# Stacks of a block-sparse cross-attention rebuilt through DRAM, with a reordered projection and the second normalization on GpSimd

## What is computed

```python
# cut to what matters; S = 512, 4 blocks of 128 per sequence, 16 heads of 16
x = _layernorm(x + causal_attention(x, Wq, Wk, Wv, Wo))             # "x1" below
Q, K, V = x @ Wq.T + bq, ctx @ Wk.T + bk, ctx @ Wv.T + bv           # per head: 512 x 16
loc_p   = softmax(Qb @ Kb.T / 4)                # a block of queries on its own block of keys
cross_p = softmax(Qb @ K[i-1, i, i+1].T / 4)    # and on the window of up to three blocks
out = loc_p @ Vb + cross_p @ V[i-1, i, i+1]
x = _layernorm(x + out @ Wo.T + bo)                                 # "x2" below
top2 gates = softmax(top_k(x @ gate_w + gate_b, 2))
x = _layernorm(x + sum_e gate_e * ffn_e(x) + ffn_shared(x))
```

## Time and profile before

| | us |
|---|---|
| median of 3 runs | 947.11 |
| lowest, highest | 946.44, 954.42 |
| the profiled execution | 951.36 |
| its span | 949.6 |

### The profile page before, as it was taken

One profiled execution on the slowest core, in us unless ns is written; L12 is line 12 of the kernel. 1 busy time (PEld: TensorE's weight loads), 2 busy tenths in 40 slices (PEclk: granted clock), 3 DMA queues, 4 the chain that ended last, 5 costly groups with the idle time before them and its releaser, 6 DMA issues. The chain is left out here.

```text
span 949.6 us, 15805 instructions
## 1 busy us (share of the span) xinstructions
PE 823.4 (87%) x5054; PEld 627.7 (66%) x5055; DVE 416.6 (44%) x766; ACT 344.3 (36%) x894; POOL 226.7 (24%) x250
## 2 busy tenths in 40 slices
PE   6584999789998789898949999899999999999940
PEld 5463867585768566765749999577777777777630
DVE  5735475657465846462457553222222222222216
ACT  2120363334352445155155431233333333333313
POOL 5902030204020210000023775411111111111116
PEclk9885999797898999899979999999999999999975
DMA  9911202130122132110073112551011111111025
GB/s 308 148 44 48 65 27 56 50 79 1 29 63 51 40 108 51 45 26 4 1 297 132 56 56 58 200 189 53 30 33 33 33 33 33 33 33 33 22 94 189
DMA packets 59127, 68.47 MB, mean 72 GB/s; under 512 B 18288, under 2 KB 43760, under 8 KB 58960
## 3 DMA queue, kind: packets, MB, share of 16 engines
q1 hardware_dynamic: 55680, 58.61, 21.7%
q0 software_dynamic: 3408, 9.34, 2.7%
HBM read 38.23 MB, written 16.59 MB: 58 GB/s over the span
## 5 line engine op out<-in xcount | busy, mean ns | idle before, releaser
L1567 PE MATMUL ps<-we,hT 128*128 x624 | 142.8, 382 | 2.5 <-ACT hT L722 2.5
L1567 PEld LDWEIGHTS ps<-we,hT 128*128 128x128 f32 x624 | 119.7, 192 | 35.5 <-issue 20.9
L1547 PE MATMUL ps<-we,xT 128*128 x312 | 140.6, 593 | 1.9 <-issue 1.9
L928 DVE TENSOR_REDUCE mx<-ps 128x4 f32<-128x512 f32 (+1 forms) x128 | 102.5, 822 | 62.5 <-PE ps L1381 61.4
L1127 DVE COPY hp<-ps 128x512 f32<-128x512 f32 x78 | 50.3, 686 | 158.4 <-PE ps L1547 158.4
L722 ACT ACTIVATE hT<-ps,b1T 128x128 f32<-128x128 f32 x312 | 84.9, 383 | 35.2 <-PE ps L1558 35.2
L1547 PEld LDWEIGHTS ps<-we,xT 128*128 128x128 f32 x312 | 56.2, 190 | 58.1 <-issue 58.1
L1381 PE MATMUL ps<-k_stack,q_stack 96*128 96x256 f32 (+1 forms) x256 | 74.2, 378 | 16.7 <-DVE mx L928 7.4
L621 ACT ACTIVATE pT<-ps 128x256 f32<-128x256 f32 x128 | 49.3, 385 | 104.4 <-PE ps L1396 96.9
L546 ACT ACTIVATE xT<-ps 128x256 f32<-128x256 f32 x39 | 14.9, 385 | 180.9 <-PE ps L1530 180.9
L1381 PEld LDWEIGHTS ps<-k_stack,q_stack 96*128 96x128 f32 x256 | 42.2, 206 | 46.2 <-issue 22.3
(11 more groups left out here) (212 smaller groups left out, 1265.5 us busy)
## 6 DMA issues: line engine op xcount, KB each, us to landing
we<-in_w SPq DMA_DIRECT2D x16, 1024.0 KB
k_stack<-k_s SPq DMA_DIRECT2D x96, 64.0 KB, 2.0
q_stack<-q_s SPq DMA_DIRECT2D x192, 32.0 KB, 2.0
slot_rows<-attn SPq DMA_DIRECT2D x1, 4992.0 KB, 25.7
xs<-slot_rows SPq DMA_DIRECT2D x39, 128.0 KB, 2.1
yl<-pair_out SPq DMA_DIRECT2D x4, 1024.0 KB, 8.9
x_raw<-in_xT SPq DMA_DIRECT2D x4, 512.0 KB, 4.0
X<-in_x SPq DMA_DIRECT2D x4, 512.0 KB, 7.1
```

Of the source, the lines that this page charges most:

```text
L928: nc.vector.tensor_reduce(mx[:, n, 2 * p:2 * p + 2, r0:r0 + nb], ps[:, 2 * (u % 2):2 * (u % 2) + 2, 0:nb * P].rearrange("p h (b k) -> p h ...
L1547: m = nc.tensor.matmul(ps[:, 2 + c, :], xT[:, q, k, :], w[:, bass.ds(e, 1), k * HID + c * 512:k * HID + (c + 1) * 512].rearrange("p o n -> ...
L1567: m = nc.tensor.matmul(ps[:, 6, 0:D], hT[:, c, :], w[:, bass.ds(e, 1), KD * HID + c * D:KD * HID + (c + 1) * D].rearrange("p o n -> p (o n)"),
```

## The change

Six things change together.

1. SP writes the high and low part of the keys and queries of a half to DRAM (`k_rows`, `q_rows`: two DMAs of 512 KB, `rows_away`) and reads the stacks back from there: 3 DMAs of 256 KB for keys, and 12 of 64 KB for queries, in two groups of two pairs. Unit 0 waits for the keys and the first six, unit 8 for the other six. The block-1 rows are written right behind the stacks of the first half.
2. `project2`: x2 is transposed late, after the third projection, and its logits come after the fourth; `turn_out` comes before the values; the 24 matmuls at its end become 10, except in the prologue.
3. DVE's statistics and its normalization of x1 are laid out row by row over the units of the second half (`norms`).
4. x2 is normalized on POOL: a subtraction, a product and the copy, each over 128 x 1024 (`norm_x2`), after the context's split.
5. Five such matmuls stand before the second half's wait for the residual sums (`WARM_G`).
6. In batch 3 the transposes of the output come ahead of x2's, and five more matmuls stand before its gates.

The core of the diff:

```diff
 WARM = 24
 WARM_B = 16
+WARM_Q = 10
+WARM_G = 5
 WARM_E = 20
 ROW = D + 2
 PARTS = ((0, 0), (0, 1), (1, 0))
 PAIRS = HALF // 2
-PAIR_DMAS = 3 + 2 * 3
+STACK_DMAS = 3 + 2 * 3
+LATE_DMAS = 2 * 3
...
-            def stack(h):
-
-                for g in range(PAIRS):
-                    for sec, part in enumerate((0, 1, 0)):
-                        sp.dma_start(k_stack[32 * sec:32 * sec + 32, h * PAIRS + g, :].bitcast(F),
-                                     k_s[32 * g:32 * g + 32, h, part, :].bitcast(F)).then_inc(stacked[g], 16)
-                    for head in (2 * g, 2 * g + 1):
+            def rows_away(b, h):
+
+                sp.wait_ge(s["qk2_lo"], 4 * b + 2 * h + 1)
+                sp.dma_start(k_rows[h].rearrange("l p t -> p l t"), k_s[:, h, :, :].bitcast(F)).then_inc(k_away[h], 16)
+                sp.wait_ge(s["qk2_lo"], 4 * b + 2 * h + 2)
+                sp.dma_start(q_rows[h].rearrange("l p t -> p l t"), q_s[:, h, :, :].bitcast(F)).then_inc(q_away[h], 16)
+
+            def stack(b, h):
+
+                sp.wait_ge(k_away[h], 16 * b + 16)
+                for sec, part in enumerate((0, 1, 0)):
+                    sp.dma_start(k_stack[32 * sec:32 * sec + 32, h * PAIRS:(h + 1) * PAIRS, :].bitcast(F),
+                                 k_rows[h, part].rearrange("(g p) t -> p g t", g=PAIRS)).then_inc(stacked[h], 16)
+                sp.wait_ge(q_away[h], 16 * b + 16)
+                for part_done, g0 in ((stacked, 0), (stacked_late, PAIRS // 2)):
+                    for par in range(2):
                         for sec, part in enumerate((0, 0, 1)):
-                            r = 32 * sec + 16 * (head % 2)
-                            sp.dma_start(q_stack[r:r + 16, h * HALF + head, :].bitcast(F),
-                                         q_s[16 * head:16 * head + 16, h, part, :].bitcast(F)).then_inc(stacked[g], 16)
+                            r = 32 * sec + 16 * par
+                            at = h * HALF + 2 * g0 + par
+                            sp.dma_start(q_stack[r:r + 16, at:at + HALF // 2 - 1:2, :].bitcast(F),
+                                         q_rows[h, part].rearrange("(g a p) t -> a p g t", g=PAIRS, a=2)
+                                         [par][:, g0:g0 + PAIRS // 2, :]).then_inc(part_done[h], 16)
...
-                sp.wait_ge(s["qk2_lo"], 4 * b + 2)
+                if not first:
+                    sp.wait_ge(stacked[1], 16 * STACK_DMAS * b)
+                rows_away(b, 0)
                 if first:
                     sp.wait_ge(s["masks"], 1)
                 else:
                     sp.wait_ge(s["b_ps"], 2 * UNITS * (2 * b - 1))
-                stack(0)
+                stack(b, 0)
+                rows_away(b, 1)
...
+                stack(b, 1)
...
-            def keep(b, c, bias):
-
-                pool.wait_ge(s["ln_out"], c + 1)
-                Xb = X[:, bass.ts(b, NT), :]
-                if bias:
-                    nc.gpsimd.tensor_tensor(Xb, res[:, 0, :, :], brow[:, 2:3, :].broadcast_to([P, NT, D]), ALU.add)\
-                        .then_inc(s["x_kept"], 1)
-                else:
-                    nc.gpsimd.tensor_copy(Xb, res[:, 1, :, :]).then_inc(s["x_kept"], 1)
+            def keep_x1(b):
+
+                pool.wait_ge(s["x1_out"], b + 1)
+                nc.gpsimd.tensor_tensor(X[:, bass.ts(b, NT), :], res[:, 0, :, :],
+                                        brow[:, 2:3, :].broadcast_to([P, NT, D]), ALU.add).then_inc(s["x_kept"], 1)
+
+            def norm_x2(g, c):
+
+                pool.wait_ge(s["ln_pow"], c + 1)
+                rows = res[:, 1, :, :]
+                nc.gpsimd.tensor_tensor(rows, rows, mv[:, :, 0:1].broadcast_to([P, NT, D]), ALU.subtract)\
+                    .then_inc(s["x2_sub"], 1)
+                pool.wait_ge(s["x2_sub"], g + 1)
+                nc.gpsimd.tensor_tensor(rows, rows, rstd[:, :].unsqueeze(2).broadcast_to([P, NT, D]), ALU.mult)\
+                    .then_inc(s["x2_out"], 1)
+                pool.wait_ge(s["x2_out"], g + 1)
+                nc.gpsimd.tensor_copy(X[:, bass.ts(g, NT), :], res[:, 1, :, :]).then_inc(s["x_kept"], 1)
...
+                if not last:
+                    norm_pow(1 if first else 2 * b)
+                    keep_x1(b + 1)
+
+                    split(c_s, c_raw, (("w1_ps", 2 * b + 4), ("c_raw_in", 16 * b + 32)), "ctx_hi", "ctx_lo", b + 1)
                 if not first:
-                    norm_pow(2 * b)
-                    keep(b - 1, 2 * b, False)
-                if not last:
-                    norm_pow(2 * b + 1)
-                    keep(b + 1, 2 * b + 1, True)
-
-                    split(c_s, c_raw, (("w1_ps", 2 * b + 4), ("c_raw_in", 16 * b + 32)), "ctx_hi", "ctx_lo", b + 1)
+                    c = 2 * b if last else 2 * b + 1
+                    norm_pow(c)
+                    norm_x2(b - 1, c)
...
-                    if j == 0 and g is not None:
-                        gate_rows(g, 0)
                     if j == 1:
                         act.wait_ge(s["ctx_lo"], b + 1)
                         for i in range(2):
                             act.wait_ge(s["v2_ps"], 2 * b + i + 1)
                             copy(v_wait[:, 2 * i:2 * i + 2, :], ps[:, 4 + i, :].rearrange("p (n d) -> p n d", n=2), "v2_out")
...
+                    if j == 2 and g is not None:
+                        gate_rows(g, 4)
...
+            def norms(u, c1, c2, done):
+
+                if u == 0:
+                    dve.wait_ge(s["ln_res"], done)
+                stats1, var1, rows1 = ((0, 1, 2, 3), 4, (6, 7, 8, 10)) if c1 is not None else ((), None, ())
+                stats2, var2 = (((5, 11, 12, 13), 14) if c1 is not None else ((0, 1, 2, 3), 4)) if c2 is not None else ((), None)
+                if u in stats1:
+                    norm_stat(stats1.index(u), 0, c1 if u == stats1[-1] else None)
+                if u in stats2:
+                    norm_stat(stats2.index(u), 1, c2 if u == stats2[-1] else None)
+                if u == var1:
+                    norm_var(c1)
+                if u == var2:
+                    norm_var(c2)
+                if u in rows1:
+                    norm_x1(rows1.index(u), c1)
...
-                    if j == 0 and g is not None:
-                        gate_logits(g, 3)
                     if j == 1 and c is not None:
                         if g is None:
                             dve.wait_ge(s["pad_out"], 32)
-                        else:
-                            gates(g, 3)
                         combine(c, 0)
+                if g is not None:
+                    gate_logits(g, 7)
+                    gates(g, 7)
...
-                half(2 * b + 1, 2 * b, 1, (() if first else ((2 * b, 1),)) + (() if last else ((2 * b + 1, 0),)))
+                glue_and_attention1(None if first else b - 1, None if last else b + 1, 1 if first else 2 * b)
+                half(2 * b + 1, 2 * b, 1, (1, None, 2) if first else (None, 2 * b, 2 * b + 1) if last
+                     else (2 * b, 2 * b + 1, 2 * b + 2))
...
-                if n is not None:
-                    pe.wait_ge(s["ln_res"], cn + 1)
-                elif cg is not None:
-                    pe.wait_ge(s["ln_res"], cg + 1)
+                if g is not None and n is not None:
+                    keep_clock(WARM_G)
+                pe.wait_ge(s["ln_res"], done)
...
-                pe.wait_ge(s["ln_out"], cn + 1)
+                pe.wait_ge(s["x1_out"], b + 1)
                 turn(4, rows_of_res(0), "x1_ps")
-                if g is not None:
-                    turn(0, rows_of_res(1), "g_ps")
                 for j, blk in enumerate((0, 0, 1, 1)):
                     if j == 0:
                         pe.wait_ge(s["ctx_lo"], b + 1)
@@ -1325,21 +1372,25 @@
                         m = mm3(pe, ps[:, 7 - j % 2, :], lambda l: w[:, 1 - j % 2, l, k, blk * P:(blk + 1) * P],
                                 lambda l: src[:, l, k, :], k == 0, k == KD - 1)
                     m.then_inc(s["qk2_ps"], 1)
-                    if j == 0 and g is not None:
-                        gate_logits(g, 3)
                     if j == 1:
-                        rows_of(4, c_s, w, 2, "v2_ps")
-                        if g is not None:
-                            gates(g, 3)
-                            pe.wait_ge(s["lgT_out"], g + 1)
                         if c is not None:
                             pe.wait_ge(s["augT_out"], c + 2)
                             turn_out(c)
-                pe.wait_ge(s["v2_out"], 2 * b + 2)
-                keep_clock(WARM)
+                        rows_of(4, c_s, w, 2, "v2_ps")
+                    if j == 2:
+                        pe.wait_ge(s["v2_out"], 2 * b + 2)
+                        if g is not None:
+                            pe.wait_ge(s["x2_out"], g + 1)
+                            turn(4, rows_of_res(1), "g_ps")
+                if g is not None:
+                    pe.wait_ge(s["qk2_lo"], 4 * b + 3)
```

(22 more changed lines are left out.)

109 lines of the change are left out of this document (56 added, 53 removed).

## The result

The changed kernel took 963.2 us (median; 961.9 to 964.4), the kernel before 948.2 beside it: a ratio of 1.0146, 95% interval 1.0096 to 1.0197. The change makes the kernel slower by about 1%; 937 was forecast. Medians and ranges here are of all executions, but a ratio counts only those within 1.5% of the kernel's fastest, which leaves out one of four of e3 and of e10, one of ten of f2 and four of ten of f4 (the profiled one among them), each 5 to 13 us above its kernel's median. The profiled execution took 962.15 us, its span is 960.4, its mean granted clock 0.897 (0.929 before).

The account below looks back on a forecast made before the run. PE, busy 87% of the span, was taken to set the time in most stages. The terms summed to -14.8 from the profiled 951.4 us: 936.6, say 937, with a range of 924 to 952.

Parts of the forecast that it names:

- Batch 0's half: First half of batch 0: no more waits for pairs, shorter aug rows, 15.4 us instead of 24.8; taken as -9.0.
- its own marks: Signs for batch 0 in the changed profile: unit 0 at 65 to 66 us, aug transposes near 81.
- Projection of batch 1: Ahead of batch 1's first half: fourteen matmuls fewer, but stacks ready only at 9.0 us; -2.0, the wait uncovered.
- First halves of batches 1, 2, 3: POOL's split of x moves ahead of the end, so all three take 22.2 us; -1.7.
- the round trip is late and the half starts cold: Rival: stacks via DRAM come at 15 us instead of 9, halves start at lower clock; 965 us, chance 0.08.
- Projections of batches 2, 3: From aug transposes to unit 0: shorter waits and fewer warm matmuls, -4.0 and -4.5, 1 added for ws; together -7.5.
- Second halves: POOL's x2 operations hold DVE's aug steps, transposes at 27.2 us: batch 1 -1.9, batch 2 +4.3; batches 0, 3 together -0.4.
- End of attention: After the last half nothing covers x2's normalization on POOL, and everything of the experts waits: +3.4.
- Glue: Stretch between the two halves of a batch, four times: forecast difference 0.

Follow-up runs that it names:

- e3: The kernel before with the stacks through DRAM alone, 24 warm matmuls kept: 942.3 us, ratio 0.9865.
- e10: The changed kernel with x2 normalized on DVE, the ws loads behind batch 3's stacks, and 10 warm matmuls: median 925.8 us, ratio 0.9732.
- f2: The changed kernel with x2's normalization on DVE alone, 10 warm matmuls and early ws loads kept: 942.9 us, ratio 0.9923.
- f4: The changed kernel with 14 warm matmuls for 10, nothing else: 949.1 us, ratio 0.9945.
- e7: The kernel before with stacks through DRAM and the two ws loads issued behind batch 3's stacks: 938.8 us, ratio 0.9855.
- f3: The changed kernel with only the ws loads moved behind batch 3's stacks: 940.4 us, ratio 0.992.
- e6: The changed kernel with 24 warm matmuls and x2 normalized on DVE, its copy staying on POOL: 939.1 us, ratio 0.9868.
- e1: The changed kernel with 24 warm matmuls again instead of 10 ahead of the first halves of batches 1 to 3: 950.0 us, ratio 1.0013.

## Why the prediction failed, step by step

**Batch 0's half** (-9.0): right, -9.3, with its own marks: unit 0 at 65.6, transposes at 81.1.

**Projection of batch 1** (-2.0): the wait was forecast as 1.3 us and was 1.5; the group came 9.6 us after SP issued the store instead of 9.0: the store was as taken, the last landing 2.5 us later, the six issues 1.5 shorter. The size was right. What it led to was not.

**First halves of batches 1, 2, 3** (-1.7, all at 22.2): this is the step that failed, by 28 us. The working counted the wait as its own length and said that it "is covered by nothing". A wait of 0.8 to 5.5 us cost its length and 9.3 more, because the half behind it ran at 1.2 GHz to its end: 31.5 us for 22.2. Part of the 9.3 comes back in the glue that follows. After h2 and h4 it took 27.6 to 28.0 us behind five of seven cold halves, 29.6 and 29.8 behind the other two, and 28.9 to 30.3 behind a warm one; after h6 20.6 to 21.0 behind a cold and 22.2 to 23.4 behind a warm one. I had the case among the rivals, "the round trip is late and the half starts cold", but asked for an idle time of 5 us, and gave it 3 us a half. Its first half, the late round trip, happened only in batch 3. The second half needs no late round trip. The sign was in the rows: the earlier trace rows showed a half at 0.53, and the earlier trace rows that it took 29.1 for 22.9. The trace has waits of 1.25, 0.70 and 1.43 us in it, and the clock fell 0.9 us behind the last. I read it as one execution's accident that the change would remove. Accident it was in part, since batch 2's half has the same three waits and stayed warm; but every such wait runs that risk, and the change put one in front of three halves.

**Projections of batches 2, 3** (-7.5): -2.5. The terms as listed take 4.5 off each, which gives 17.9 for batch 2 and not the 18.4 that was written. Batch 2 took 19.0. Batch 3 took 23.7, because the store behind 2 MB of loads landed after 8.4 us; 1 us was allowed for it. e7 and f3 show it: with the loads behind the stacks the wait is gone.

**Second halves** (-1.9, +4.3): -3.3 and +2.9, right in kind. Both took 25.8 us for the 27.2 taken, mainly since POOL's subtraction and product take 1.90 us, and not the 2.37 of a sum of the same size. One aug step was caught by each, as the working had it, and the low clock of h3 did not come back. e6 prices the lock by taking POOL's operations away: 3.3 us a half. The Trainium skill, "SBUF — State Buffer", section "SBUF: two separate sides", has the rule that the prediction used: the engine that comes second to the shared port pair waits for the whole operation of the first. DVE's rows of 2.06, 1.88 and 1.85 us, each with its POOL row, agree.

**End of attention** (+3.4): +4.0; 3.2 of it goes when x2 is back on DVE (e6). PE waits 2.5 us for POOL there, and part of the rest is clock: x2's transposes and logits behind the wait take 1.62 and 1.04 us, for 1.06 and 0.62 before.

**Glue** (0): -6.3, not foreseen, 3.2 and 2.7 of it behind the cold h2 and h6: the mean clock there is 1.00, where it was 0.87 and 0.86 before. Behind the cold h4 it is 0.90 for 0.91, and the glue 0.2 longer. Where it comes, it is the other side of the same cost.

Without the cold halves the sum would have held roughly: +10.8 less 28.3 for the halves, and 3 to 5 back for the glue (an estimate from the two ranges above), is -14.5 to -12.5 against -14.8. That is partly luck: the projections of batches 2 and 3 were 5.0 us worse than forecast, and the second halves 2.9 better and the glue 1 to 3. e1 alone doesn't reach it, since it pays for 14 more matmuls and keeps the wait in batch 3.

What stays open: what decides between full and half clock after a wait of 1.3 to 1.7 us. The Trainium skill, "TensorE: Matmul & The Clock Gate", section "What's actually happening", says of a kernel's start that the same kernel can show different numbers of slow matmuls from run to run. No run here looks at that start, but f2 and f3 show the like behind a wait: one warm and one cold at the same place of the same program. Whether the row of warm matmuls ahead of a wait of under 1 us matters (0.83 us fell behind ten, 0.85 behind fourteen and 0.73 and 0.93 behind twenty did not) is not settled by single halves. Nor is it settled whether the burst of DMA makes a fall more likely: at waits of about 1.5 us 6 of 8 halves fell with it, 3 of 8 without, at other places of the program.
